# An attention and mixture-of-experts layer on one core: the order of work ahead of the first expert units, and fewer groups of score products

## What is computed

```python
x = x + attn(cond(x))
x = x + ffn(cond2(x))
# cond: per sequence, softmax over masked scores of tanh(x W1 + b1) v, pools x; divided by the mask's count
# attn: 16 heads of 8, plus one shared rotary part of 32, causal softmax over 32 keys, output product W_o
# cond2: x @ W[cat] + b[cat], one of 64 matrices for each sequence
# ffn:
scores = sigmoid(x @ gate_w.T)            # 64 experts, the best 8 out of the best 4 groups
y += cw[:, e] * ((silu(x @ wg[e]) * (x @ wu[e])) @ wd[e])     # for all 64 experts, cw is 0 where not chosen
y += (silu(x @ Ws_gate) * (x @ Ws_up)) @ Ws_down
```

## Time and profile before

| | |
|---|---|
| median of 3 runs | 755.12 us (753.29 to 757.13) |
| profiled execution | 754.2 us, span 752.4 us |
| TensorE busy in the span | 721.2 us (96%) |
| VectorE, ScalarE, GpSimd busy | 547.1, 453.3, 425.5 us |
| the chain that ended last | PE 75%, ACT 9%, DVE 8%, POOL 4%, issue 2%, DMA 1% |
| unit 0 of block 0 starts | 69.65 us |

### The profile page before, as it was taken

How to read it: one execution, slowest core, us unless ns; L and a number is a source line. 1 busy time by engine, 2 the same in 40 slices (tenths; PEclk the granted TensorE clock), 3 DMA queues, 4 the chain that set the end, 5 groups by cost and what they waited for, 6 DMA issues and landing times.

```text
span 752.4 us, 15834 instructions
## 1 busy us (share of the span) xinstructions
PE 721.2 (96%) x5644; PEld 556.2 (74%) x5644; DVE 547.1 (73%) x1150; ACT 453.3 (60%) x872; POOL 425.5 (57%) x349
## 2 busy tenths in 40 slices
PE   4788989999999999999999999999999999999997
PEld 3576767777787777777787777777777777877885
DVE  3867666886688856976778866888569766886664
ACT  2656875477555775567655775556755675555553
POOL 2456864555455655566455664566456555566665
PEclk8899999999999999999999999999999999999999
DMA  7494344434454364444545345443644344345451
GB/s 262 143 340 116 112 123 113 138 98 127 121 117 134 103 142 112 128 112 117 121 128 131 102 144 121 105 121 109 151 114 131 105 122 126 100 124 148 127 135 47
DMA packets 69055, 97.20 MB, mean 129 GB/s; under 512 B 8017, under 2 KB 26897, under 8 KB 68977
## 3 DMA queue, kind: packets, MB, share of 16 engines
q1 hardware_dynamic: 64512, 91.21, 44.8%
q10 hardware_dynamic: 4464, 4.98, 1.9%
HBM read 90.73 MB, written 4.98 MB: 127 GB/s over the span
## 4 chain that ended last, share of the span: by engine, by line
PE 75%; ACT 9%; DVE 8%; POOL 4%; issue 2%; DMA 1%; POOLq 0%; DVEq 0%; SPq 0%; ACTq 0%
PE Y L950 21%; PE U L950 20%; PE G L950 20%; PE A L950 12%; POOL hid_lo L613 2%; ACT s_t L378 2%; DVE act_w L921 2%; ACT hid_hi L517 2%; ACT L505 1%; DVE hid L933 1%; PE A L1011 1%; ACT L378 1%; ACT G L505 1%; DMA pooled_scratch<-hid 1%; DMA w<-in_weights 1%
## 5 line engine op out<-in xcount | busy, mean ns | idle before, releaser
L613 POOL TENSOR_TENSOR hid_lo<-hid,hid_hi 128x512 fp32r<-128x512 f32 (+1 forms) x264 | 342.2, 1296 | 277.5 <-ACT hid_hi L517 276.7
L921 DVE TENSOR_TENSOR act_w<-G,cwb 128x512 f32<-128x512 f32 x248 | 170.4, 687 | 99.8 <-ACT G L505 98.0
L505 ACT ACTIVATE G<-G 128x512 f32<-128x512 f32 x248 | 144.4, 582 | 149.3 <-PE G L950 147.5
L517 ACT CAST hid_hi<-hid 128x512 fp32r<-128x512 f32 (+1 forms) x264 | 162.3, 615 | 64.3 <-DVE hid L933 63.5
L933 DVE TENSOR_TENSOR hid<-act_w,U 128x512 f32<-128x512 f32 (+1 forms) x256 | 175.7, 686 | 23.4 <-PE Y L950 1.5
L950 PE MATMUL G<-c_hi,wg_hi 128*128 128x512 f32 x248 | 113.6, 458 | 0.0
L950 PE MATMUL Y<-hid_hi,wd_hi 128*128 128x512 f32 (+1 forms) x264 | 106.6, 404 | 5.3 <-POOL hid_lo L613 5.0
L950 PE MATMUL Y<-hid_hi,wd_lo 128*128 128x512 f32 (+1 forms) x264 | 103.5, 392 | 0.0
L950 PE MATMUL Y<-hid_lo,wd_hi 128*128 128x512 f32 (+1 forms) x264 | 103.5, 392 | 0.0
L950 PE MATMUL U<-c_hi,wu_hi 128*128 128x512 f32 x248 | 98.4, 397 | 0.0
L950 PE MATMUL G<-c_hi,wg_lo 128*128 128x512 f32 x248 | 97.7, 394 | 0.0
(11 more groups left out here) (183 smaller groups left out, 894.7 us busy)
## 6 DMA issues: line engine op xcount, KB each, us to landing
cwb<-cw_scratch SPq DMA_DIRECT2D x256, 256.0 KB, 3.7
k_blk<-in_cond_w SPq DMA_DIRECT2D x112, 64.0 KB, 2.3
wg_raw<-in_we_gate SPq DMA_DIRECT2D x8, 256.0 KB, 6.1
wu_raw<-in_we_up SPq DMA_DIRECT2D x8, 256.0 KB, 6.2
wd_raw<-in_we_down SPq DMA_DIRECT2D x8, 256.0 KB, 6.7
xf<-in_x_feat SPq DMA_DIRECT2D x8, 256.0 KB, 4.2
out_feat<-y ACTq DMA_DIRECT2D x8, 256.0 KB, 2.2
h_feat<-pooled_scratch SPq DMA_DIRECT2D x7, 256.0 KB, 2.7
```

The costliest lines, as they stand in the source:

```text
L505: nc.scalar.activation(gate_bank(p)[:, :], gate_bank(p)[:, :], ACT.Silu).then_inc(S["silu_done"], 1)
L517: nc.scalar.copy(hid_hi[0:n, p % NH, :], hid[0:n, p % NH, :]).then_inc(S["hi_ready"], 1)
L613: nc.gpsimd.tensor_sub(hid_lo[0:n, p % NH, :], hid[0:n, p % NH, :], hid_hi[0:n, p % NH, :].bitcast(F32)).then_inc(S["lo_ready"], 1)
L921: nc.vector.tensor_mul(act_w[:, p % NH, :], gate_bank(p)[:, :], cwb[:, p % NCW, :])\
```

## The change

It concerns block 0 and the order around it, and one thing in every block.

- Block 0's probabilities are turned tile by tile: ScalarE alternates exponential and copy in step 10, and the transposes go to bank G1 and wait for their own tile's exponential alone.
- The scores of pooling blocks 1 to 3 are formed before block 0's first products, those of 4 to 7 behind the first attention tile; `pool_weights`, `spread`, `pool_out` and `pooled_out` are in other places, up to `pool_out(7)` inside unit 0.
- 14 matmuls on zeroed memory stand first on TensorE; the identity matmuls are distributed anew.
- Splits 7 to 16 lie together ahead of unit 0, and the eight others in units 11 to 18 (before: units 0 to 7). ScalarE calls silu once on one column before unit 0. The waits for the stored pooled blocks are moved from ScalarE's unit 0 to its unit 9 (block 6) and are VectorE's alone for blocks 5 and 7.
- In every block q is computed ahead of k; the four value products stand together in step 5 (block 0: step 2); the score products of two tiles each stand together in steps 6 and 8.

```diff
-        WARM = {0: 4, 9: 6, 12: 2, 13: 2, 14: 2, 15: 2, 16: 2, 17: 2, 20: 2, 21: 20}
+        SPLIT_UNITS = range(11, 11 + NSPLIT + 1 - BEFORE_UNITS)
+        WARM_BLANK = 14
+        WARM = {9: 4, 12: 2, 13: 2, 14: 2, 15: 2, 21: 24}
...
+                elif p == EXPS and opening(blk):
+                    for t in range(TILES):
+                        act.wait_ge(S["sub_tile"], t + 1)
+                        nc.scalar.activation(s_t[:, t, :], s_t[:, t, :], ACT.Exp, scale=ATT_SCALE)\
+                            .then_inc(S["prob_tile"], 1)
+                        if t >= 1:
+                            turned_probs(t - 1, 0)
+                    turned_probs(TILES - 1, 0)
...
-                    split(p - 14)
-            for i in range(5, NBLK):
-                pooled_out(i)
+                    split(p - 16)
+                    if p == 30:
+                        for i in range(15, BEFORE_UNITS):
+                            split(i)
+                        nc.scalar.activation(small[:, 8:9], small[:, 8:9], ACT.Silu)
...
-                if not prev and BEFORE_UNITS + p <= NSPLIT:
-                    split(BEFORE_UNITS + p)
+                if not prev and p in SPLIT_UNITS:
+                    split(BEFORE_UNITS + p - SPLIT_UNITS[0])
                 if p == 0 and not prev:
-                    for i in range(5, NBLK):
-                        act.wait_ge(S[f"h_stored{i}"], 16)
+                    pooled_out(7)
+                if p == X2_MOVED and not prev:
+                    act.wait_ge(S["h_stored6"], 16)
...
+            pool_scores(1)
 
             rotate(0)
...
-                if p == 4:
-                    pool_scores(1)
-                elif p == 9:
+                if p == 13:
                     pool_scores(2)
+                elif p == 16:
                     pool_weights(1)
-                elif p == 16:
                     spread(1)
+                elif p == 18:
                     spread(2)
-                elif p == 18:
                     pool_weights(2)
...
+                mm(A2[:, :], W["q"], h_feat[:, :]).then_inc(S["q_ps"], 1)
                 mm(A1[:, :], k_w[:, :], h_feat[:, :]).then_inc(S["k_ps"], 1)
-                mm(A2[:, :], W["q"], h_feat[:, :]).then_inc(S["q_ps"], 1)
...
-                elif 6 <= p < 10:
-                    t = p - 6
...
+                elif p in (6, 8):
+                    for t in (p - 6, p - 5):
...
+            pe.wait_ge(S["pt_blank"], 1)
+            for _ in range(WARM_BLANK):
+                mm(U[1][:, 0:P], spread_p[:, 0, 0:P], spread_p[:, 0, 0:P])
...
-            warm(4)
             pool_hidden(0)
+            warm(2)
...
+            warm(2)
+            pool_scores(1)
+            warm(6)
             pool_out(0)
             pe.wait_ge(S["setup"], 2)
+            warm(2)
             first_products(0)
-            pool_scores(1)
             pool_hidden(2)
...
-                elif p in (17, 18):
-                    pool_out(p - 16)
+                elif p == 18:
+                    pool_out(1)
+                elif p == 20:
+                    pool_out(2)
...
+            first_products(1)
             pool_out(5)
-            first_products(1)
             pool_out(6)
-            pool_out(7)
...
+                if p == 0 and not prev:
+                    pool_out(7)
```

More of the change, by code:

```diff
@@ L478, in _ @@
                     pool_exp(1)
-                elif p == 10:
+                    split(2)
+                    split(3)
+                elif p == EXPS:
                     pool_exp(2)
@@ L970, in attention_step @@
                         first_products(blk + 1)
-                elif p == 2:
-                    pe.wait_ge(S["rot_ready"], blk + 1)
-                    for t in range(TILES - 1):
-                        mm(A0[:, bass.ts(t, P)], h_feat[:, bass.ts(t, P)], v_w[:, :])
+                elif p == 2 and opening(blk):
+                    value_products(blk)
                 elif p == 5:
+                    if not opening(blk):
+                        value_products(blk)
                     pe.wait_ge(S["q_ready"], blk * NG + NG)
@@ L1021, in attention_step @@
                             pe.wait_ge(S["weighted"], blk * NPAIR + LENT + 1)
[L1022 removed]
+                    elif t == 1 and opening(blk):
+                        pe.wait_ge(S["biased_tile"], TILES - 1)
+                    elif t == 1:
                         pe.wait_ge(S["hid_ready"], (blk - 1) * UNITS + LENT + 1)
```

76 lines of the change are left out of this document (39 added, 37 removed).

## The result

The changed kernel takes **748.76 us**, median of 4 runs (748.12 to 749.39), against 755.16 before (4 runs): ratio 0.9915, 95% interval 0.9887 to 0.9942. In a second session it took 748.11 (6 runs) against 756.10 (17 runs): 0.9885, 0.9865 to 0.9906. It is faster, but by 6.4 to 8.0 us, not by 15.2, and it lies outside the range: 8.9 us above the forecast of 739.9. The profiled execution took 748.2 us, span 746.4, to be set against the 739.0 of my own sum: 9.2 us are missing.

What follows compares the result with a forecast made beforehand. TensorE was taken to bound later blocks and an engine chain the first 100 us. The prologue and block 0's -10.9 plus later blocks' -4.3 made -15.2 on 754.2: 739.0, or 739.9 against the median; range 735 to 746.5.

Steps and rivals of the forecast that it cites:

- What bounds the kernel now: Later blocks: TensorE is the bound, busy 84.45 of 85 us; first 100 us: a chain from engine to engine.
- Part 1: Head, to block 0's first product: zeros raise the clock early, so 17.05 becomes 15.1, -2.0 us.
- Part 2: To the first score tile: rope product and rotation come sooner, first score product at 23.2 instead of 27.49, -4.3 us.
- Part 3: Attention of block 0: tile-by-tile transposes bring the result's transposes to 36.1 instead of 43.43, -7.3 us.
- Part 4: To block 1's first products: start at 56.4 instead of 63.70, -7.3 us, despite warm-ups, splits and table load.
- Part 5: Block 1 and units 0 to 8: -11.9 us, less 1.0 taken back for one fall of the clock, -10.9.
- the sentence on the splits in units 11 to 18: Moved splits: GpSimd has 2.5 us a unit there against TensorE's mean 2.7, and nobody needs one before unit 20.
- Part 6: Blocks 2 to 7: paired scores save 0.64 and grouped value products 0.1 us a block; 4.4 in six, taken as -4.3.
- the zeros did lift the clock: Rival at the head: the zeros don't lift the clock, or one step later; head 1.8 late, 742 us, chance 18%.
- the pairs did gain: Rival in later blocks: no gain, VectorE ends the second tile late each time; +4.3, 744 us, chance 14%.
- the transfer: Rival at the prologue's tail: pooled block 7's store holds VectorE, +2.4, up to 6 with weight loads; 746 us, 11%.
- three signs of being wrong: Clock 0.50 between 12 and 22 us; TensorE awaiting VectorE's maximum in later blocks; GpSimd's low part as releaser, units 11 to 20.

Runs made afterwards that it cites:

- the run on the tail: Changed kernel with 19 instead of 24 warm-up products ahead of the routing weights' transposes and ScalarE's table load moved behind its copy of cw_feat: 746.37 us.
- the run on the held splits: Changed kernel with GpSimd's splits 4 to 6 of the prologue held until the pooling weights of group 1 are spread: 746.62 us against 748.11.
- the five edits: Changed kernel with values all at step 2, splits in units 7 to 14, prologue splits held, two stands filled, shorter warm-up and later table load: 741.28 us.
- the last version: The five edits together plus twelve more warm-up products in each of two stands, ahead of c2's transposes and the last but one pooling product: 740.82 us.

## Why the prediction was wrong

**What bounds the kernel now:** right. **Part 1, -2.0:** right in its result (15.00 for 15.1), and the clock did rise under the zeros (28 records in 5.20 us, the next product at full pace). But 17.05 would have become 16.44 without them, and the closeness is in part luck: how soon the clock rises differs from one execution to the next, the 28 records take 4.87 to 6.20 us in the ten profiles that have them, and 15.00 is the earliest rope product of the ten.

**Part 2, -4.3:** right, -4.7. **Part 3, -7.3:** -6.0. The step that failed is a silent one: it walked on from 23.2 with the full clock for the first 64 score records, 1.96 us. They took 3.53 behind a stand of 1.75 us that the walk itself contained. I had put 1.0 us aside for one fall (in part 5), and named this stand; the fall costs 1.1 to 1.7 (3.03 to 3.64 us in seven profiles), and the profiled execution of the second session had two.

**Part 4, -7.3:** -5.3 at the first products. The costs that it named came as described (64 warm-up records, table load ahead of the copy; the run on the tail takes 1.7 to 2.4 us off the kernel), but it has no term for VectorE's two products on the pooling scores growing (0.17 to 0.61 and 0.56 to 1.31 us) because the change puts GpSimd's splits beside them. Missed: 1.5 us by the run on the held splits.

**Part 5, -10.9:** -5.3. Here lies the first large failure, the sentence on the splits in units 11 to 18: it compared GpSimd's 2.5 us a unit with TensorE's 2.7 and asked who reads the splits. They cost 3.2 us in units 20 to 24 by holding VectorE's routing; the run with that edit alone shows the gain and the loss side by side, 3.1 (2.6 with unit 9) and 3.2. The gain of GpSimd's relief in units 0 to 6 didn't come, 0.1 us longer in that run. The walk up to unit 5 was 2.3 us short in the profiled execution, of which the pause is 1.65; in other executions the wait for the maximum, up to 2.55, takes its place.

**Part 6, -4.3:** the pairs were right, 4.1 in six blocks alone; the margin of VectorE held. The second large failure is the value products, forecast at 0.1 us gained a block and measured at 0.3 to 0.5 lost, 2.2 us in all as an edit alone and 3.7 to 4.3 when taken back. The estimate priced the switch between groups and its bounds, 0 and 0.2, had no loss in them, though no row excluded one. The records' own 0.67 us moved unchanged from units 30 and 31, ahead of TensorE's wait for the last `hid`, to behind it in unit 0, and the wait that they had filled (0.28 us in the rows shown) came on top.

**The rivals.** The forecast was likelier than each of them and none is what happened: the zeros did lift the clock, the pairs did gain, the transfer cost nothing that shows in the first profile, and 0.5 to 2.55 us in six others, up to the rival's 2.4 but not its 6. None of the three signs of being wrong shows in the profile either: they watched other places. The two mechanisms that made the miss were in none. The sum: 1.8 us missing at unit 0 (clock and GpSimd), 3.2 in units 20 to 24, 3.6 in the later blocks, and some 0.6 left between, in which the pause, the 1.0 set aside and the 0.66 that the value products give back in units 30 and 31 of block 0 stand against each other. This is a sum over one execution; another of the same kernel starts unit 0 2.7 us later. The runs confirm the parts, but they don't add up exactly: the five edits taken alone give 1.5 to 4.4 us each, 11 to 14 in all, and 6.8 to 7.5 together. Where their gains in block 0 overlap isn't shown; the waits for transfers (1.18 us at 57.56 in the last version) and the clock are the candidates.

## What to carry to other kernels

Ask of a moved instruction not only who needs its result, but what its engine holds while it runs: here, GpSimd's two-input instruction beside VectorE's two-input instruction on SBUF. Work on the bounding engine that stands ahead of a wait costs its time less that wait; moved behind the wait, it costs all of it. And count an early rise of the clock only together with the stands behind it: here the medians gave 2.1 us for it with those filled and nothing without.

## What the runs showed of the hardware

- VectorE's instructions with two SBUF inputs end 0.03 to 0.42 us after the GpSimd instruction that they start beside: 0.17 became 0.61, 0.28 became 1.39, 0.56 became 1.31 us. In the changed kernel's profile that holds for 30 of 35; the other five, of 0.18 us and starting within 0.13 us of GpSimd's, pass it. Those that read one input from PSUM (`hid<-act_w,U`, at most 0.69) stay as they are.
- The granted clock fell behind stands of 1.55, 1.75 and 1.95 us, and didn't fall behind a stand of 1.75 us at the same place in the kernel without zeros: the length of the stand alone doesn't decide it. At the stand of 1.55 us near 42 it fell in one of the changed kernel's two profiles and not in the other.
- A fall costs 1.6 us at a group of 64 records (3.53 against 1.96; 3.03 to 3.64 in seven profiles), and executions of one kernel at a mean clock of 0.998 and 0.994 lie 2.4 us apart. The clock isn't all of that: the version with every stand filled has 0.998 to 1.000 and takes 740.3 to 741.5, not 738.9.
- TensorE had single pauses of 0.89 to 1.65 us with nothing in the trace that it waited for, in two of the profiles: twice in the first score pair of block 1, once in the last ones of block 0.
